# Three of an expert's four lower products from rounded halves, in all eight chunks

## The reference, cut to what matters

```
a = softmax(q k^T / sqrt(H)) v @ Wo + bo        # in groups of 128 tokens
x = x + a
gates = softmax(x @ Wg + bg)
hmid  = relu(einsum("bsh,ehd->bsed", x, W1) + b1)   # 8 experts, 128 -> 512
eout  = einsum("bsed,edh->bseh", hmid, W2) + b2     # 512 -> 128
y     = einsum("bse,bseh->bsh", gates, eout)
```

## Time and profile before

| | |
|---|---|
| median of 3 runs | 1016.47 us (1015.79 to 1018.13) |
| the profiled execution's own time | 1018.25 us |
| its span, first to last instruction | 1016.5 us |
| mean granted clock of TensorE | 0.956 of full speed |
| PE busy | 924.7 us (91%) |
| DVE busy | 712.3 us (70%) |
| ACT busy | 635.6 us (63%) |
| POOL busy | 365.2 us (36%) |

### The profile page before, as it was taken

The page is one execution under the profiler, slowest core; times in us unless marked ns, Lnnn a source line. Parts: engine busy times, 40 slices in busy tenths (PEclk is TensorE's granted clock), DMA queues, the critical chain, the costliest instruction groups (busy, mean ns, idle before and its releaser), DMA issues.

```text
span 1016.5 us, 17880 instructions
## 1 busy us (share of the span) xinstructions
PE 924.7 (91%) x6484; PEld 658.1 (65%) x6484; DVE 712.3 (70%) x1858; ACT 635.6 (63%) x1097; POOL 365.2 (36%) x442
## 2 busy tenths in 40 slices
PE   4597988999997999999999999999989897988997
PEld 3354545555675878866666676766767666877983
DVE  8977877777487767875868778677776767842314
ACT  4477667777785667667766676776765564533420
POOL 4356062132001111245334454334451441367770
PEclk9588988998998999999999999999999998998999
DMA  5853244436591000011101111120113222122316
GB/s 136 212 147 104 66 126 124 125 105 196 146 203 64 22 23 22 2 43 43 62 22 42 43 63 41 32 73 22 40 45 129 59 75 70 42 60 71 100 49 223
DMA packets 86403, 83.15 MB, mean 82 GB/s; under 512 B 9202, under 2 KB 72680, under 8 KB 86316
## 3 DMA queue, kind: packets, MB, share of 16 engines
q1 hardware_dynamic: 81092, 73.32, 25.7%
q0 software_dynamic: 4320, 8.27, 2.4%
q10 hardware_dynamic: 904, 0.42, 0.1%
HBM read 50.53 MB, written 31.72 MB: 81 GB/s over the span
## 4 chain that ended last, share of the span: by engine, by line
PE 64%; DVE 21%; SPq 5%; issue 4%; ACT 3%; DMA 2%; POOL 1%; another core or an unknown queue 0%; DVEq 0%; POOLq 0%; ACTq 0%
PE psum L1568 17%; PE psum L1610 8%; PE psum L1591 6%; PE psum L1605 5%; PE psum L1404 4%; PE psum L1342 3%; DVE maxes L1984 3%; DVE pieces L2105 2%; PE psum L1358 2%; SPq L1182 2%; PE psum L1385 1%; PE psum L1312 1%; PE psum L1525 1%; PE psum L1418 1%; PE psum L1482 1%
## 5 line engine op out<-in xcount | busy, mean ns | idle before, releaser
L1568 PE MATMUL psum<-parts,q_stack 128*128 128x512 f32 x640 | 255.3, 480 | 10.5 <-DVE parts L2307 5.7
L2600 ACT ACTIVATE big<-psum,cols 128x512 f32<-128x512 f32 x207 | 140.9, 686 | 91.4 <-PE psum L1568 84.2
L1568 PEld LDWEIGHTS psum<-parts,q_stack 128*128 128x128 f32 x640 | 114.9, 193 | 71.2 <-issue 46.6
L2825 POOL TENSOR_TENSOR hT<-hT,gb_tok 128x512 f32<-128x512 f32 x54 | 75.0, 1389 | 231.0 <-DVE gb_tok L2120 230.5
L1568 PE MATMUL psum<-parts,k_stack 128*128 128x512 f32 x320 | 127.6, 399 | 0.0
L1984 DVE TENSOR_REDUCE maxes<-psum 128x4 f32<-128x1024 f32 (+1 forms) x96 | 114.0, 1216 | 17.4 <-PE psum L1358 17.0
L1610 PE MATMUL psum<-big,ew 128*128 128x512 f32 x240 | 122.7, 594 | 0.0
L1605 PE MATMUL psum<-pieces,w_parts 128*128 128x512 f32 x336 | 101.6, 410 | 0.0
L2898 POOL DMA_INDIRECT routed<-big,slot_i x64 | 65.6, 1025 | 62.5 <-DVE slot_i L2294 34.6
L2105 DVE TENSOR_TENSOR pieces<-big,pieces 128x512 fp32r<-128x512 f32 x87 | 71.0, 823 | 23.5 <-ACT pieces L2607 17.0
L2921 POOL DMA_INDIRECT answers<-hT,to x64 | 62.8, 982 | 55.3 <-DVE hT L2322 37.8
(11 more groups left out here) (434 smaller groups left out, 1927.2 us busy)
## 6 DMA issues: line engine op xcount, KB each, us to landing
gb_tok<-gate_rows SPq DMA_DIRECT2D x32, 512.0 KB
q_stack<-q_pieces SPq DMA_DIRECT2D x32, 192.0 KB, 3.4
k_stack<-k_pieces SPq DMA_DIRECT2D x32, 192.0 KB, 4.4
routed<-empty_row SPq DMA_DIRECT2D x4, 1040.0 KB, 13.4
big<-routed SPq DMA_DIRECT2D x16, 260.0 KB
answers<-gb_tok SPq DMA_DIRECT2D x4, 1024.0 KB, 11.1
q_pieces<-gb_tok SPq DMA_DIRECT2D x16, 192.0 KB, 2.1
k_pieces<-gb_tok SPq DMA_DIRECT2D x15, 192.0 KB, 2.1
```

The costliest lines, as they stand in the source:

```text
L1568: last = eng.matmul(bank(i), w1_part(wp, e)[:, fs], parts[2 * xk + xp][:, :], start=n == 0, stop=n == 2)
L2600: eng.activation(slots[held("slot", "up", n, e, f)], bank(held("bank", "up", n, e, f)), ACT.Relu, bias=col("L0_ffn_b1", e * FC + f)).then_ ...
L2825: eng.tensor_tensor(hT[:, ns], xpT[:, ns] if e == 0 else hT[:, ns], gate_wide[:, e // GHELD % 2, e % GHELD, :], ALU.add).then_inc(sem("acc ...
```

## The change

`SPLIT` becomes (0, 1, 2), and `cut_in_two` no longer leaves out the last chunk: 192 of the 256 lower products are made from halves (112 before), 80 more. The low halves of W2 are written in place over the raw blocks 0 to 2 in `ew2` (`w2_low`); the high halves take 3/4 of `ew1` (`w2_high`), and the last quarter of `ew1` becomes a fourth set of pieces. Since `ew1` is now used until the last chunk, the transfer of the second layer's w1 becomes eight of 256 KB, each waiting for the lower products of chunk 7 whose high halves lie under it (`under_w1`: experts 1, 2, 3, 5, 6, 7, 7, 7 for e = 0 to 7). The half of `hid` over pieces 0 and 1 comes free after chunk 7 in place of chunk 6.

```diff
@@ -37,7 +37,7 @@
 
 
 GHELD = 2
-SPLIT = (0, 1)
+SPLIT = (0, 1, 2)
 KS = len(SPLIT)
 BEHIND, BEHIND_CUT, BEHIND_LAST = 2, 6, 3
 MASKED = -1e30
@@ -137,7 +137,15 @@
 
 def cut_in_two(n, f):
 
-    return n < NCH - 1 and f in SPLIT
+    return f in SPLIT
+
+
+MORE_PIECES = (NE - 2, NE - 1)
+
+
+def under_w1(e):
+
+    return min(NE - 1, (FF * (e + 1) - 1) // (KS * C))
 
 
 def down_order(n):
@@ -656,20 +664,23 @@
                 p.step("acc", n, e, work="pool:1.4", urgent=60 if n == NCH - 1 else 0, after=[("mix", n, e)] + ([("acc", n, e - 1)] if e else []))
         add_mixed(n, MOE - 300, (20 + n, -1, 0))
     for e in range(NE):
-        p.step("sv", e, work="act:.42 dve:.45", after=[("sw", 0, e), ("bg", 2), ("bg", 3)]
+        p.step("sv", e, work="act:.53 dve:.57", after=[("sw", 0, e), ("bg", 2), ("bg", 3)]
                + ([(("up", 0, e - 1, 0), "pe")] if e else []))
     third = [("wt", 4), last_pv]
     p.step("third_over", after=third, then=found("pieces", (2,), ((("wt", 4), "pe"), (last_pv, "pe"))))
-    p.step("w1", work="sp:.1 dma:12", after=[("down", NCH - 2, e, SPLIT[-1]) for e in range(NE)])
-    for half, pool, ids, last in ((1, "pieces", (0, 1), [("down", NCH - 2, e, f) for e in range(NE) for f in SPLIT]),
+    p.step("more_pieces", after=[("sw", 0, e) for e in MORE_PIECES],
+           then=found("pieces", (3,), (*((("sw", 0, e), "dve") for e in MORE_PIECES),)))
+    for e in range(NE):
+        p.step("w1", e, work="sp:.5 dma:3", after=[("down", NCH - 1, under_w1(e), SPLIT[-1])])
+    for half, pool, ids, last in ((1, "pieces", (0, 1), [("down", NCH - 1, e, f) for e in range(NE) for f in SPLIT]),
                                   (0, "slot", range(4), [("down", NCH - 1, e, f) for e in range(NE) for f in range(FC)])):
         old = [p.buffer(pool, i) for i in ids]
         p.step("free", "hid", half, work="sp:0", after=last, opens=[(0, b) for b in old],
                then=lambda now, half=half, old=old: p.pools["hid"].update({half: sum((b.before for b in old), ())}))
     for e in range(NE):
-        p.step("sw", 1, e, work="act:.6 dve:.69", after=[("w1",), (("up", NCH - 1, e, FC - 1), "pe")])
+        p.step("sw", 1, e, work="act:.6 dve:.69", after=[("w1", e), (("up", NCH - 1, e, FC - 1), "pe")])
     for h in range(4):
-        p.step("w2", h, work="sp:.5 dma:4", after=[(("down", NCH - 1, 2 * h + 1, FC - 1), "pe")]
+        p.step("w2", h, work="sp:.5 dma:4", after=[(("down", NCH - 1, 2 * h + 1, SPLIT[-1]), "pe")]
                + ([("fetch", u) for u in range(2)] if h == 3 else []))
 
     p.step("wraw", work="sp:10 dma:6", after=[*values_over, ("mrow", B - 1)])
@@ -904,8 +915,8 @@
         q_in = [semaphore(f"q_in{i}") for i in range(QR)]
         k_in = [semaphore(f"k_in{i}") for i in range(QR)]
         m_in = [semaphore(f"m_in{i}") for i in range(QR)]
-        qk_in, fill_out, ew_in, ew1_in = (
-            semaphore(n) for n in ("qk_in", "fill_out", "ew_in", "ew1_in"))
+        qk_in, fill_out, ew_in = (semaphore(n) for n in ("qk_in", "fill_out", "ew_in"))
+        ew1_in = [semaphore(f"ew1_in{e}") for e in range(NE)]
         ew2_in = [semaphore(f"ew2_in{i}") for i in range(4)]
         raw_in, blk_in, blk_zero, columns, gates_out = (semaphore(n) for n in ("raw_in", "blk_in", "blk_zero", "columns", "gates_out"))
         gates_in = [semaphore(f"gates_in{i}") for i in range(2)]
@@ -1047,8 +1058,10 @@
         slots = [*(big2[:, k * CHUNK:(k + 1) * CHUNK] for k in range(4)), sb("slot4", [P, CHUNK])[:, :]]
         halves = [*(rounded(f"pieces{k}{h}", CHUNK, "big2", NT * VAW, (4 + 2 * k + h) * CHUNK) for k in range(2) for h in range(2)),
                   rounded("pieces20", CHUNK, "m_pieces", 2 * 2 * S // 2),
-                  rounded("pieces21", CHUNK, "big1", NT * VW, TOK)]
-        w2_parts = rounded("w2_parts", NE * FF, "ew1", NE * FF)[:, :].rearrange("p (e h k c) -> p e h k c", e=NE, h=2, c=C)
+                  rounded("pieces21", CHUNK, "big1", NT * VW, TOK),
+                  *(rounded(f"pieces3{h}", CHUNK, "ew1", NE * FF, MORE_PIECES[h] * FF) for h in range(2))]
+        w2_high = rounded("w2_high", NE * KS * C, "ew1", NE * FF)[:, :].rearrange("p (e k c) -> p e k c", e=NE, c=C)
+        w2_low = rounded("w2_low", NE * FF, "ew2", NE * FF)[:, :].rearrange("p (e k c) -> p e k c", e=NE, c=C)[:, :, 0:KS, :]
         ROWS_AT = 2 * FC * CHUNK
         rows_buf = big2[:, ROWS_AT:ROWS_AT + 2 * TPB * TOPK * ROW].rearrange(
             "p (r t k n) -> p r t k n", r=2, t=TPB, k=TOPK)
@@ -1217,14 +1230,13 @@
                 eng.dma_start(gate_wide[:, h % 2, :, :], gate_rows[n, GHELD * h:GHELD * (h + 1), :].unsqueeze(0).to_broadcast(
                     [P, GHELD, CHUNK])).then_inc(gates_in[h % 2], 16)
 
-            def w1():
-                for e in range(NE):
-                    w.wait_ge(*done("down", NCH - 2, e, SPLIT[-1]))
-                eng.dma_start(ew1[:, :, :], a["L1_ffn_w1"].rearrange("e p f -> p e f")).then_inc(ew1_in, 16)
+            def w1(e):
+                w.wait_ge(*done("down", NCH - 1, under_w1(e), SPLIT[-1]))
+                eng.dma_start(ew1[:, e, :], a["L1_ffn_w1"][e]).then_inc(ew1_in[e], 16)
 
             def w2(h):
                 es = slice(2 * h, 2 * h + 2)
-                w.wait_ge(*done("down", NCH - 1, 2 * h + 1, FC - 1))
+                w.wait_ge(*done("down", NCH - 1, 2 * h + 1, SPLIT[-1]))
                 eng.dma_start(ew2[:, es, :, :], a["L1_ffn_w2"][es, :, :].rearrange("e (k p) c -> p e k c", p=P)).then_inc(
                     ew2_in[h], 16)
 
@@ -1601,8 +1613,8 @@
                     k, kx = held("pieces", "down", n, e, f), SPLIT.index(f)
                     w.wait_ge(*done("hs", n, e, f))
                     w.wait_ge(*done("sv", e))
-                    for m, (wp, xp) in enumerate(((0, 0), (0, 1), (1, 0))):
-                        last = eng.matmul(bank(i), w2_parts[:, e, wp, kx, :], halves[2 * k + xp][:, :],
+                    for m, (w2_part, xp) in enumerate(((w2_high, 0), (w2_high, 1), (w2_low, 0))):
+                        last = eng.matmul(bank(i), w2_part[:, e, kx, :], halves[2 * k + xp][:, :],
                                           start=f == order[0] and m == 0, stop=f == order[-1] and m == 2)
                 else:
                     w.wait_ge(*done("up", n, e, f))
@@ -2094,7 +2106,7 @@
 
             def sv(e):
                 w.wait_ge(*done("sv", e, by="act"))
-                eng.tensor_tensor(w2_parts[:, e, 1, :, :], ew2[:, e, 0:KS, :], w2_parts[:, e, 0, :, :].bitcast(F32),
+                eng.tensor_tensor(w2_low[:, e, :, :], ew2[:, e, 0:KS, :], w2_high[:, e, :, :].bitcast(F32),
                                   ALU.subtract).then_inc(sem("sv"), 1)
 
             def hs(n, e, f):
@@ -2580,7 +2592,7 @@
                     for u in range(6):
                         w.wait_ge(*done("exp", 12 + e // 2, u, by="pe"))
                 else:
-                    w.wait_ge(ew1_in, 16)
+                    w.wait_ge(ew1_in[e], 16)
                     w.wait_ge(*done("up", NCH - 1, e, FC - 1, by="pe"))
                 eng.copy(w1_part(0, e), ew1[:, e, :]).then_inc(sem("sw", "act"), 1)
 
@@ -2609,7 +2621,7 @@
             def sv(e):
                 w.wait_ge(*done("sw", 0, e))
                 w.wait_ge(ew_in, 16 * 4)
-                eng.copy(w2_parts[:, e, 0, :, :], ew2[:, e, 0:KS, :]).then_inc(sem("sv", "act"), 1)
+                eng.copy(w2_high[:, e, :, :], ew2[:, e, 0:KS, :]).then_inc(sem("sv", "act"), 1)
 
             def up2(u, f):
                 w.wait_ge(*done("up2", u, f, by="pe"))
```

## The result

The changed kernel took 1019.0 us (median of 12 runs, 1014.88 to 1027.37), the kernel before 1015.72 us beside it. The ratio is 1.0039, with a 95% interval of 1.0023 to 1.0056: slower by 0.39%, 4.0 us. The profiled execution had a span of 1018.5 us. Its own time was 1020.2 us, 1.2 us above the median; the one before, with 1018.25 us, was 2.5 us above its median. So the two traces show about half of the 4.0 us.

A forecast was written before the change was run, and what follows sets the result against it. TensorE was taken as the main but not only bound, with VectorE on the chain too. Subtraction costs less TensorE's savings, plus the turn, gave +8.0 us whole, -2.2 half, middle +2.9: 1019.4 us, range 1015 to 1024 (eight in ten: 1006 to 1029).

The forecast's parts named there:

- The total: Whole kernel: 2.9 us slower, the middle of +8.0 and -2.2, so 1016.47 becomes 1019.4 us; chance 0.36.
- TensorE's gain: All chunks: 80 exchanged products save 13.6 us of TensorE, of which 9.7 us shortens the chain (shares 66% and 84%).
- The price of a subtraction: VectorE's L2105: each new subtraction costs 0.26 us, its share of the chain in chunks 2 to 6.
- the half case: Whole kernel: new subtractions cost half of 0.26 us each, and the sum comes to -2.2 us.
- Rival A's point of decision: Whole kernel: the change is faster if a new subtraction costs less than (9.7 + 2.6 - 1.35) / 80 = 0.14 us.
- Rival A: Whole kernel faster, 1008 us: TensorE is the bound and the new plan hides the cutting; chance 0.30.
- ScalarE at nothing: ScalarE's 80 added roundings of 0.62 us cost nothing, covered by its idle time; 2.4 us if that cover were gone.
- Chunks 0 and 1: Experts' first two chunks: 16 new subtractions cost 1.0 us (0.5 at half price), less 1.8 us saved on TensorE.
- Chunks 2 to 6: Experts' middle chunks: 40 subtractions cost 10.4 us (5.2 at half price), less 4.5 saved; 1 to 6 us over 302.9.
- rival C: VectorE saturates in chunk 7, which takes over 66 us; whole kernel 1029 us; chance 0.14.
- Chunk 7: Last experts' chunk: 24 subtractions 6.2 us, less 2.6 moved out and 3.4 TensorE: +0.2 us, or -2.9 at half price.
- The turn: Between last lower product and first unit: four moved subtractions on VectorE add 2.7 us, or 1.35 at half price.

The follow-up runs named there:

- four pairs of orders: Both kernels replanned with a subtraction booked at 0.66, 0.72, 0.80, 0.90 us, same instructions; ratios before 1.0041, 1, 1.0035, 0.9889; changed 1.0093, 1.0039, 1.0024, 1.0136.
- short rounding: Changed kernel, same order, ScalarE's rounding of block 2 on 8 columns in place of 512 in chunks 1 to 7; ratio 1.0045 to the kernel before.
- two-block kernel: Changed kernel with SPLIT back at (0, 1) in all eight chunks, new layout and late w1 kept; ratio 1.0032 to the kernel before.
- chunk 7 plain: Changed kernel with chunk 7's lower products plain again and w1 loaded after chunk 6; ratio 1.0033, 1021.37 us beside 1017.83 for the kernel before.

## Why the forecast came out, point by point

- **The total**, 1019.4 us, came within 0.4 us of the measured 1019.0. It was counted from 1016.47 us, the kernel before having 1015.72 in the later comparison, so that it was +2.9 us against a measured +4.0. It was a sum of terms of which some were wrong, and other orders of the same instructions put it anywhere from 1018 to 1030 us (1.0024 to 1.0136 of 1015.72). The direction was argued; the size was luck to a good part.
- **TensorE's gain**, 9.7 us from 13.6, was over-sized: 46% of its time counts and not 66 to 84%, 6.3 us.
- **The price of a subtraction**, 0.26 us at the whole and 0.13 us at the half, measured 0.09 us with its order held. Read as a share of the chain it was far too high, and the half case was the nearer one. For 80 of them that is 7.3 us. Both terms shrink together, which fits two paths of nearly the same length. The difference of the two, +1.0 us, has the sign that I gave and a quarter of the measured 4.0 us; an interval of 3 us on either side makes it no proof.
- **Rival A's point of decision**, 0.14 us a subtraction, is passed (0.09), yet the kernel is slower. The step that fails there is the 9.7 us on the other side of that sum: with 6.3 us the point of decision is 0.09 us, and the sum comes to no change. Rival A's time of 1008 us also leaves out the 2.6 us that its own point of decision counts; with them it is 1005.5 us.
- **ScalarE at nothing**: borne out by the short rounding.
- **Chunks 0 and 1**, forecast at -0.8 us: wrong. All four pairs of orders show them longer, by 4.8 us in the mean, 3.2 us when counted from the first upper product. I took the absence of L2105 from the chain's named lines as a low price for new ones. In the profile after, it holds 7.3 us of the chain there, more than the 2.7 us that TensorE saves at most. The two-block kernel, without the third block in these chunks, shows none of the loss (187.2 us). Which part of the third block it is, the 16 subtractions, the larger `sv` (put at nothing) or the order around them, is open: no run took out one of them alone.
- **Chunks 2 to 6**, forecast +3.3 us: -3.2 us in the profile, and not settled over the orders. By the mark that I set for the forecast being wrong (under 300 us, rival A), this stretch went rival A's way: 299.7 us. The total fits all the same, so its agreement says little for this mechanism.
- **Chunk 7**: forecast between -2.9 and +0.2, and rival C's saturation. VectorE was busy for 53.55 of 63.1 us (85%); putting the chunk back changed the total by 0.6 us. Rival C's sign, over 66 us, did not come in any of the four orders (59.7 to 63.1 us).
- **The turn**, +1.4 to +2.7 us: it grew by 5 us, nearly all of it by another cause, GpSimd's `acc` behind two routed transfers and a granted clock of 0.50 under the small products. It is no matter of one order: from the last `mix` to the first `up2` the four orders before take 12.3 to 17.0 us, the four changed ones 18.9 to 22.7, and the kernels with chunk 7 plain and with two blocks 22.2 and 21.9. The clock falls to 0.50 between 1.1 and 3.1 us after the last `mix` in the four changed orders, and not before 14.2 us after it in the four others. Part of it came back in the units, so that what stays is 2.0 us in the mean of four orders. I had taken every delay of the first `up2` as a delay of the end; this was wrong.

## What to carry to other kernels

When an engine's list is fixed by a planner, draw the order a few times, by a planned duration that changes no instruction, before crediting a change of half a per cent to the change: here that alone moved the time by 1.5%, and gave a faster kernel than the edit under study. A share of the chain is a poor price: the subtraction's 0.26 us was 0.09 us when it was taken away, because a second path stood just behind, and `acc`, with 2.6 us on the named chain, gave 7.6 us. In this kernel, with the two engines 91% and 70% busy, the exchange is close to even. Such an exchange is best priced by shortening each of the two instructions in place, with the order held.

## What the runs showed of the hardware

In the turn of the changed kernel, eight small f32 products took 2.07 us behind an idle 2.81 us, at a granted clock of 0.50; in the kernel before they took 1.16 us at 1.00. The idle time alone does not decide it. In the kernel with two blocks, the same eight products came behind an idle 3.04 us and took 1.16 us, at 1.00; the clock fell to 0.50 only under the next ones (first line: its first 1.2 us of small products; second: what follows):

```profile
835.50:836.70 1.20, 1.20 (x10) 1.20 (x11) 0.00 (x0) 1.20 (x3) 0.89 (x2) 1.00 1.11 290
837.00:840.30 3.30, 3.30 (x17) 3.30 (x17) 2.27 (x9) 3.30 (x8) 1.94 (x2) 0.50 0.53 198
```

In the changed kernel the clock fell at 838.25, 1.1 us after TensorE's last lower product had ended and with one earlier idle stretch, of 0.63 us, ahead of its last three.

GpSimd's additions of 128x512, shortened to 8 columns, took 15.8 us off VectorE's 250.63 us in chunks 2 to 6, though no instruction of VectorE was changed.

The last of the final transfers (512 KB) took 10.65 us in one profile and 8.97 us in the other, with the same requests before it: 1.7 us of the 2.0 between the two spans, and nothing that the other traces repeat.
